# Fill of the slot table moved to the sync queue; normalisation roots of the node stage moved from VectorE to GpSimd

## The reference, cut to what matters

```python
h = maximum(layernorm(x), 0)                      # per node
skip_s, skip_v = s @ W_skip0, v @ W_skip1         # from h, per node
s, v = s @ W_nl0, v @ W_nl1
w = relu(edge_feature @ W_fc1) @ W_fc2            # per edge
xs, xv = s[dst], v[dst]                           # gather per edge
tp = [w0*xs, w3*dot(xv, sh1), w1*xs*sh1, w2*xv, w4*cross(xv, sh1)]
agg = segment_sum(tp, src) / 32                   # scatter per edge
out_s = agg_s @ W_out_s + skip_s
out_v = agg_v @ W_out_v + skip_v
out = x + [silu(out_s[:64]), sigmoid(out_s[64:96]) * out_v]
```

## Time and profile before

| | |
|---|---|
| runs | 1316.05, 1317.16, 1323.12 us; median 1317.16 |
| profiled execution | 1322.71 us, of which span 1320.8 us |
| PE, DVE, ACT, POOL busy | 84%, 78%, 66%, 33% of the span |
| transfers | 271.10 MB, mean 205 GB/s |

### The profile page before, as it was taken

One profiled execution on the slowest core, in us unless ns is written; L12 is line 12 of the kernel. 1 busy time (PEld: TensorE's weight loads), 2 busy tenths in 40 slices (PEclk: granted clock), 3 DMA queues, 4 the chain that ended last, 5 costly groups with the idle time before them and its releaser, 6 DMA issues.

```text
span 1320.8 us, 29100 instructions
## 1 busy us (share of the span) xinstructions
PE 1114.8 (84%) x8847; PEld 938.2 (71%) x8847; DVE 1026.3 (78%) x4002; ACT 865.9 (66%) x2070; POOL 442.2 (33%) x410
## 2 busy tenths in 40 slices
PE   5003998999999999989698999888998889988996
PEld 4002666888888888778577777777777777777775
DVE  8004998898888889776487888888888888888875
ACT  0003012787788778565677888788887888878884
POOL 6777710578787877777200000000000000000000
PEclk9556998999999999798699999999999999999998
DMA  9998200344544475444476677767777677666762
GB/s 358 406 406 308 66 23 9 91 132 133 130 130 135 129 244 176 122 114 123 128 256 241 246 265 255 252 230 262 257 259 259 222 264 256 250 252 239 261 213 108
DMA packets 108457, 271.10 MB, mean 205 GB/s; under 512 B 13573, under 2 KB 51751, under 8 KB 108364
## 3 DMA queue, kind: packets, MB, share of 16 engines
q1 hardware_dynamic: 76396, 194.15, 42.7%
q0 software_dynamic: 19200, 36.48, 9.4%
q10 hardware_dynamic: 12768, 39.34, 7.5%
HBM read 126.91 MB, written 143.01 MB: 204 GB/s over the span
## 4 chain that ended last, share of the span: by engine, by line
PE 35%; DVE 20%; issue 13%; POOL 13%; ACTq 8%; ACT 6%; DMA 2%; DVEq 0%; SPq 0%; POOLq 0%
POOL slots L505 9%; PE bank L1452 9%; ACTq L1135 8%; DVE n_stat L903 5%; DVE ob L994 4%; POOL xg L495 4%; PE bank L1465 4%; ACT nn L1233 4%; PE bank L1444 4%; PE bank L1284 3%; PE bank L1381 3%; PE bank L1456 2%; PE bank L1410 2%; DMA xb<-x 2%; PE bank L1316 2%
## 5 line engine op out<-in xcount | busy, mean ns | idle before, releaser
L1233 ACT ACTIVATE nn<-xb,n_bias,n_rstd 128x160 f32<-128x160 f32 x784 | 346.0, 526 | 87.8 <-DVE n_bias L634 87.8
L505 POOL DMA_INDIRECT slots<-msg,sidx x200 | 230.3, 1152 | 135.6 <-DVE sidx L758 71.4
L903 DVE BATCH_NORM_STATS2 n_stat<-xb 128x6 f32<-128x160 f32 x784 | 203.1, 314 | 11.9 <-DMA xb<-x 11.6
L994 DVE SCALAR_TENSOR_TENSOR ob<-sg,bank 128x128 f32<-128x128 f32 x588 | 132.7, 281 | 97.0 <-ACT ob L1248 95.8
L1452 PE MATMUL bank<-fwd,nt 128*128 128x160 f32 x784 | 146.5, 310 | 67.0 <-DVE ob L994 66.1
L1465 PE MATMUL bank<-mg,hot 64*128 64x192 f32 x1568 | 173.3, 340 | 9.2 <-DVE hot L979 9.2
L1452 PEld LDWEIGHTS bank<-fwd,nt 128*128 128x128 f32 x784 | 113.0, 191 | 81.4 <-issue 61.1
L495 POOL DMA_INDIRECT xg<-x,dst_i x136 | 148.6, 1093 | 44.1 <-issue 38.6
L1240 ACT ACTIVATE nt<-bank 128x640 f32<-128x640 f32 x196 | 137.2, 700 | 22.3 <-PE bank L1445 18.2
L1444 PE MATMUL bank<-ident,nn 128*128 128x128 f32 x784 | 147.0, 311 | 2.6 <-ACT nn L1233 2.6
L1001 DVE TENSOR_TENSOR ob<-ob,xb 128x1280 f32<-128x1280 f32 x98 | 146.0, 1490 | 2.6
(11 more groups left out here) (181 smaller groups left out, 2399.7 us busy)
## 6 DMA issues: line engine op xcount, KB each, us to landing
xb<-x SPq DMA_DIRECT2D x97, 640.0 KB, 5.1
out_dram<-ob SPq DMA_DIRECT2D x97, 640.0 KB, 3.3
slots<-blank ACTq DMA_DIRECT2D x14, 2744.0 KB
mg<-slots SPq DMA_DIRECT2D x98, 392.0 KB, 4.0
messages<-msg SPq DMA_DIRECT2D x50, 382.8 KB
ef<-edge_feat_t SPq DMA_DIRECT2D x50, 125.0 KB
slots<-msg,sidx POOLq DMA_INDIRECT x200, 4.3
xg<-x,dst_i POOLq DMA_INDIRECT x136, 6.8
```

The lines of the kernel that those rows point to most:

```text
L505: pool.indirect_dma_start(slots[:, :], bass.IndirectOffsetOnAxis(ap=sidx[:, m:m + 1], axis=0), msg[:, c, t, 0:MW], None).then_inc(e_sc[c], 16)
L903: done = dve.bn_stats(n_stat[:, u // U, u % U * G + g, :], xb[:, u, g, :])
L994: last = dve.scalar_tensor_tensor(out=o[:, :, S + V * j:S + V * j + V], in0=sg[:, h, :, :], scalar=1.0, in1=z[:, :, part], op0=ALU.add, op ...
L1233: last = act.activation(nn[:, u % 2, h, spread_of(g % 4)], xb[:, u, g, order_of(g % 4)], ACT.Relu, bias=n_bias[:, u // U, c:c + 1], scale= ...
```

## The change

The fill goes from ACT's list to SP's, behind the first four loads of edge features, and the weight loads go from SP's list to the head of ACT's. On ACT the square root comes before the zeros for `msg`. On DVE the clearing of `blank` comes after that of the weight tiles. PE's wait for `s_fwd` goes from step 30 to step 60. `FIRST_GATHERS` is 104 and the order of later gathers follows a new `due`. In the node stage the roots and shifts of all blocks but the first four are made by POOL, with a power of -1/2 in place of seed and Newton steps; DVE's statistics are split in two halves of four around `gate(i, u, 0)`; ACT's `norm` waits for the shift of its own block.

```diff
-    FIRST_GATHERS = 132
+    FIRST_GATHERS = 104
...
 SyncE
-                sp.wait_ge(s_clr, 1)
-                for to, of in weight_loads:
-                    sp.dma_start(to, of).then_inc(s_w, 16)
...
                 for q in range(ER):
                     load_f(q)
+                sp.wait_ge(s_blank, 2)
+                for k in range(NM // FILL):
+                    rows = slots[k * (FILL * BPM * P):(k + 1) * (FILL * BPM * P), :]
+                    sp.dma_start(rows.rearrange("(b p k) c -> p b (k c)", p=P, k=BPM),
+                                 blank[:, 0:BPM * MW].unsqueeze(1).to_broadcast((P, FILL, BPM * MW))).then_inc(s_fill, 16)
...
 GpSimd
-                    due = min(NT, max(FIRST_GATHERS + 3 * (p + 1) // 2, GE * (p + 12)))
+                    due = min(NT, max(FIRST_GATHERS + 2 * (p + 1), GE * (p + 10)))
...
+                    def spread(j, w):
+                        b, base = w // U, 2 * (j - U)
+                        stat, sums = n_stat[:, b, :, :], n_sum[:, b, :, :]
+                        pool.wait_ge(n.stats, min(j + U, NM) if isinstance(j, int) else j + U)
+                        pool.tensor_tensor(sums[:, 0, :], stat[:, :, 1], stat[:, :, 4], ALU.subtract)
+                        pool.tensor_tensor(sums[:, 1, :], stat[:, :, 2], stat[:, :, 5], ALU.add).then_inc(n.chain, 1)
+                        pool.tensor_tensor(sums[:, 2, :], stat[:, :, 1], stat[:, :, 4], ALU.add).then_inc(n.spread, U)
+                        pool.wait_ge(n.chain, base + 1)
+                        pool.tensor_tensor(sums[:, 3, :], sums[:, 0, :], sums[:, 0, :], ALU.mult)
+                        pool.tensor_scalar(sums[:, 1, :], sums[:, 1, :], 1.0 / F, EPS, ALU.mult, ALU.add).then_inc(n.chain, 1)
+                        pool.wait_ge(n.chain, base + 2)
+                        pool.sem_inc(s_held, 1)
+                        pool.tensor_scalar(sums[:, 3, :], sums[:, 3, :], 0.25, None, ALU.mult).then_inc(n.chain, 1)
+                        pool.wait_ge(n.chain, base + 3)
+                        pool.tensor_tensor(sums[:, 4, :], sums[:, 3, :], sums[:, 1, :], ALU.add).then_inc(n.chain, 1)
+                    def root(v, w):
+                        k, b = w % U, w // U
+                        base, cols = 2 * (v - k - U), slice(w % U * G, w % U * G + G)
+                        pool.wait_ge(n.chain, base + 4 + k)
+                        wait(pool, n.norm, 2 * (v - XU) + 2)
+                        pool.tensor_tensor(n_rstd[:, b, cols], n_sum[:, b, 4, cols], neg_half[:], ALU.pow
+                                           ).then_inc(n.chain, 1)
+                        pool.tensor_scalar(n_sum[:, b, 2, cols], n_sum[:, b, 2, cols], -0.5, None, ALU.mult
+                                           ).then_inc(n.half, 1)
+                        pool.wait_ge(n.chain, base + 5 + k)
+                        pool.wait_ge(n.half, v - U + 1)
+                        pool.tensor_tensor(n_bias[:, b, cols], n_sum[:, b, 2, cols], n_rstd[:, b, cols], ALU.mult
+                                           ).then_inc(n.ln, 1)
+                    def round_n(i, u):
+                        v, w = i + 2, (u + 2) % XU
+                        if macro_exists(v) and macro_exists(i - 2):
+                            if w % U == 0:
+                                spread(v, w)
+                            root(v, w)
...
 VectorE, round of the node stage (the rest of the removed chain is cut)
-                            shift_n(j, w)
+                        if measure:
+                            stats_n(s, v, 0, 4)
                         if every:
                             places(i)
                         gate(i, u, 0)
+                        if measure:
+                            stats_n(s, v, 4, 8)
...
 ScalarE
-                act.wait_ge(s_blank, 2)
-                for k in range(NM // FILL):
...
+                act.wait_ge(s_clr, 1)
+                for to, of in weight_loads:
+                    act.dma_start(to, of).then_inc(s_w, 16)
...
-                        act.wait_ge(n.ln, i - u % U + U)
+                        act.wait_ge(n.ln, i + 1)
...
 TensorE
-                    if t == 30:
+                    if t == 60:
                         pe.wait_ge(s_fwd, 1)
```

More of the change, by code:

```diff
@@ L254, in __init__ @@
                 self.root = sem(f"{name}_root")
+                self.stats = sem(f"{name}_stats")
+                self.spread = sem(f"{name}_spread")
+                self.chain = sem(f"{name}_chain")
+                self.half = sem(f"{name}_half")
                 self.ln = sem(f"{name}_ln")
@@ L531, in _ @@
+                pool.wait_ge(s_half, 1)
+                nodes(main)
                 pool.wait_ge(b_fin, 1)
@@ L557, in _ @@
                 last.then_inc(s_clr, 1)
+                dve.memset(blank[:], 0.0).then_inc(s_blank, 1)
                 dve.memset(zeros_w[:], 0.0)
+                dve.memset(neg_half[:], -0.5).then_inc(s_half, 1)
                 dve.memset(ones_h[:], 1.0)
@@ L901, in stats_n @@
                             dve.wait_ge(n.x[u], earlier(i, u, XU, 16) + 16)
+                            if u % U == 0:
+                                wait(dve, n.spread, i - XU)
                         for g in range(first, last):
                             done = dve.bn_stats(n_stat[:, u // U, u % U * G + g, :], xb[:, u, g, :])
-                        if last == G and (u % U == U - 1 or isinstance(i, int) and i == NM - 1):
-                            done.then_inc(n.root, 1)
+                        if last == G:
+                            done.then_inc(n.stats, 1)
                     def level(i, u):
@@ L922, in squares @@
                         sums = n_sum[:, b, :, :]
-                        dve.wait_ge(n.root, base + 2)
+                        dve.wait_ge(n.root, base + 1)
                         dve.tensor_tensor(sums[:, 3, :], sums[:, 0, :], sums[:, 0, :], ALU.mult)
@@ L936, in halve @@
                         b, base = u // U, level(i, u)
-                        dve.wait_ge(n.root, base + 4)
+                        dve.wait_ge(n.root, base + 3)
                         dve.tensor_scalar(n_seed[:, b, :], n_sum[:, b, 4, :].bitcast(I32), 1, None,
@@ L950, in root_a @@
                         y = n_rstd[:, b, :]
-                        dve.wait_ge(n.root, base + 7)
+                        dve.wait_ge(n.root, base + 6)
                         dve.tensor_tensor(n_step[:, b, 0, :], y, y, ALU.mult).then_inc(n.root, 1)
@@ L962, in root_c @@
                         y = n_rstd[:, b, :]
-                        dve.wait_ge(n.root, base + 9)
+                        dve.wait_ge(n.root, base + 8)
                         dve.scalar_tensor_tensor(out=y, in0=n_step[:, b, 1, :], scalar=1.5, in1=y,
@@ L1131, in _ @@
             def _(act):
+                act.wait_ge(s_clr, 1)
+                for to, of in weight_loads:
+                    act.dma_start(to, of).then_inc(s_w, 16)
+                act.wait_ge(s_tab, 1)
+                act.activation(vec_r[:], vec_d2[:], ACT.Sqrt).then_inc(s_sqrt, 1)
                 act.wait_ge(s_blank, 2)
-                for k in range(NM // FILL):
-                    rows = slots[k * (FILL * BPM * P):(k + 1) * (FILL * BPM * P), :]
-                    act.dma_start(rows.rearrange("(b p k) c -> p b (k c)", p=P, k=BPM),
-                                  blank[:, 0:BPM * MW].unsqueeze(1).to_broadcast((P, FILL, BPM * MW))).then_inc(s_fill, 16)
                 for c in range(MR):
```

60 lines of the change are left out of this document (10 added, 50 removed).

## The result

The changed kernel takes 1211.99 us (median of 4 runs, 1209.00 to 1218.37) against 1319.81 us of the kernel before in the same comparison: a ratio of 0.919, with a 95% interval of 0.914 to 0.924. The prediction's median was 1204. Its sum for the profiled execution was 1207, and that execution took 1209.0 us. The two gains in that sum were mis-sized in opposite directions, which the rest of this text takes apart.

A forecast was written before the change was run, and what follows sets the result against it. Bins wait for ACT's fill issue, POOL's list sets the edge stage, DVE's chain of roots delays the node stage. 1322.7 less 46 (edges) and 69 (nodes) gives 1207, median 1204; own range 1166 to 1245, eight in ten 1168 to 1268.

The forecast's parts named there:

- The stop in the bins: Bins: the 90.4 us stop goes whole; weights scaled from about 40 us on, with some seven us in hand.
- The gathers: Edge stage: first scatter at 152.9, last gather at 532.2, last scatter landed at 598.0 against 644.3, a gain of 46 us.
- The tail behind it: Edge stage: from last gather's landing to last scatter's landing, 61.9 us as before.
- half of the 90 us is given back: Edge stage: 36 more issues stand on POOL's list behind the first scatter, so half the bins' gain is lost.
- Roots to POOL: Node stage: PE's floor 23.6 us plus 0.8 loss make 24.4 us for four blocks, a gain of 69 us.
- the free time: Node stage: POOL's chain may take 6.1 us before PE loses time, 3.7 plus 2.4 that ACT makes good.
- The price from the page: Node stage, POOL: 0.13 us for 32 elements; nothing would be lost and the time some 20 us below the sum.
- The split of the statistics: Node stage: moves half of DVE's statistics behind the gate product PE waits for; costed at nothing, covered by ACT's gates.
- The sum: Whole kernel: 1322.7 less 46 and 69 is 1207 for the profiled execution; median put at 1204.
- The rivals: Three: node stage unchanged, 1271 us, 0.10; weights late in the bins, 1262, 0.08; POOL slow in node stage, 1386, 0.10.
- a scatter's price: Node stage rival: ten POOL operations at 0.99 + 0.30 us plus a residual, 14.4 us; 1386 us, chance 0.10.
- The weights did not wait for the fill: Bins rival, negated here: weight loads on ACT's queue land only when the fill ends, near 106; 1262 us, chance 0.08.

The follow-up runs named there:

- wait30: The changed kernel with PE's wait for the scaled weights at step 30 again instead of 60: 1223.94 us, ratio 0.926 to the kernel before.
- old_gathers: The changed kernel with 132 first gathers instead of 104 and the old order of later gathers: 1192.57 us, ratio 0.903 to the kernel before.
- pow_cheap: The changed kernel with a product in place of POOL's power, leaving out the root: 1187.45 us, ratio 0.901 to the kernel before.
- blockwise: 132 first gathers and old gather order, with POOL's chain made for each block once its statistics are there: 1167.53 us, ratio 0.886 to before.
- pow_twice: The changed kernel with each power on POOL made twice, first into a spare tile: 1249.46 us, ratio 0.948 to the kernel before.
- stats_first: The changed kernel with DVE's first half of statistics ahead of the residual and one-hot rows: 1462.31 us, ratio 1.109 to before.
- three_scatters: 132 first gathers and old gather order, with only three of each group's four scatters, leaving out messages: 1154.01 us, ratio 0.879 to before.

## Why the prediction was right, and where its steps were not

**The stop in the bins.** Right. It went whole, the loads were issued and the weights scaled by 37.9 us against the "40 on" of the text, and 8.1 us of cover were in hand where it said seven. wait30 shows what the later place of PE's wait is worth: 11 us of PE's time, 12 us of the kernel's, and nothing with the old gathers.

**The gathers.** The size came out within the bounds, 54 us for 46; the reason was wrong. The first scatter came at 147.8 for 152.9 and the last gather at 530.7 for 532.2. The tail behind it was taken over from before as 61.9 us and was 590.27 - 533.25 = 57.0, with 36 scatters left in it instead of 44; with 1.4 us less for the last landing that makes the gain 54 instead of 46. From the first scatter to the last gather were 530.75 - 147.82 = 382.9 us for the 379.3 of the sum, so the arithmetic held. The step that fails is the account given of it, "half of the 90 us is given back: 36 more issues stand on POOL's list behind the first scatter". POOL has 400 issues whatever their order. What could be gained here was POOL's own stop, 71.4 us, not the 90.4 of DVE and PE, and the part not gained is the idle time that is left: that stop fell by 61.4 us, POOL's waits for messages grew by 1.2 beyond their ordinary gaps, and its issues took 445.7 us in all instead of 440.0, which makes 54.5 for the 54. POOL's busy time is the figure in front of (x403) in these windows of before and after, which end with its last scatter:

```profile
4.00:641.50 637.50, 518.97 (x3969) 434.45 (x3969) 471.44 (x1954) 329.45 (x715) 439.98 (x403) 0.88 0.53 169
4.00:586.95 582.95, 525.77 (x3969) 439.38 (x3969) 471.25 (x1954) 328.63 (x714) 445.66 (x403) 0.93 0.58 186
```

old_gathers, with no idle time, gained 72. The prediction's text says that POOL's list sets the edge stage and then counts only from the first scatter on; the list runs from the first gather.

**Roots to POOL.** The mechanism was right: PE's rate is the floor, POOL's chain is late by a little, once in four blocks. The floor holds: without the loss the node stage gained 83.7 (pow_cheap) and 85 us (blockwise, against the earlier trace rows), where the bound said 89. The loss is then 24 to 27 us in 24.5 periods, about 1.06 us for 0.8. Two terms made it, and that their errors nearly met is luck. The chain of 5.8 us lies in the stated 5.6 to 7.4, but is made up otherwise: eight operations at 0.20 to 0.57 us (the 0.57 in part a hold beside DVE's one-hot rows, 0.30 where DVE stood) instead of 0.41, one hold of some 1.1 instead of 1.49, and a power of 1.67 that no row had shown. And the free time was mis-sized: of the 6.1 us, the 3.7 are right (ACT would have begun at 809.31 - 2.06 = 807.25, which is 3.77 behind the chain's start), but ACT makes good about 1.0 us of its wait, not 2.4: it waited 2.06 and 1.06 were lost; in pow_twice it waited 3.65 and 26.38 - 23.6 = 2.8 were lost. The signs say the same: PE's waits for the gate product almost went, as forecast, and ACT's wait for the shift was 2.06 us where "about 1 us or less" was to show it.

**The price from the page.** The estimate of 0.13 us from "GPSIMD Engine Reference" of the Trainium skill (Performance versus the Vector engine) was half of what L544 and L548 took where nothing held them, 0.28 and 0.24 us. The measurement decides: the 20 us that it would have given did not come.

**The split of the statistics** was costed at nothing, and was not tried alone; nor was the new condition of ACT's `norm`, which waits for its own block's shift. stats_first shows that the place of the statistics is not free in general.

**The sum.** -54 for -46 and -60 for -69 cancel to 1209 for 1207; that the sum came so close is luck. The 5.5 us by which the median was put below the profiled execution did not come again: here it lies 3 us above. 1207 less 5.5 is 1202 and not the 1204 of the text, and the lower node gain of 38 us in the range is worked out nowhere: the stated loss of 1.3 us gives 57.

**The rivals.** None came. POOL's operations are not at a scatter's price, except the power. The weights did not wait for the fill.

## What to carry to other kernels

Where one engine issues every transfer by index, add up its whole list, from its first issue to its last, and its idle time; a stop elsewhere is worth only what that engine stands idle for, and moving its issues about gains nothing once it never stands. When work goes to an idle engine, ask when it is due rather than how dear it is: the same roots cost some 26 us when made for four blocks just in time, and nothing measurable when made block by block, in 40 operations for four blocks instead of 19, a few blocks ahead. Before an operation is moved forward, look for what it waits for and what its release lets start, or a load that was hidden closes a ring.

## What the runs showed of the hardware that was not expected

- A power on POOL took 1704 ns for 128x8 elements, eight times the 207 ns that a product in its place took (pow_cheap).
- A POOL operation of 0.22 us stretched to 1.36 us beside a DVE residual with two SBUF inputs and ended with it, while the residual took 1499 ns on average, for 1490 in the kernel before, where POOL did nothing in this stage.
- Where PE waits for gathered rows its granted clock is lower: 0.85 of full speed on average from 400 to 509 us in old_gathers, so part of the stretch at 1.2 instead of 2.4 GHz. In three_scatters, where PE was busy for 107.71 of the same 109 us, it is 1.00.
